# Two-layer transformer on one core: in its last stage, comparisons move to GpSimd and products and Gelus change places

## The reference, cut to what matters

```python
def _L1_ffn_ref(inputs, bn_gamma, bn_beta, w_q, keys_p, down, up):
    ...                                  # xn: inputs normed over all rows
    q = (xn @ w_q.T).reshape(b, s, 2, NH, KD).transpose(2, 0, 1, 3, 4)
    sim = jnp.einsum('pbnhd,hkpd->pbnhk', q, keys_p)
    scores, idx = jax.lax.top_k(sim, K)
    all_scores = (scores[0][..., :, None] + scores[1][..., None, :]).reshape(b, s, NH, K * K)
    all_idx = (idx[0][..., :, None] * NK + idx[1][..., None, :]).reshape(b, s, NH, K * K)
    sc, pk = jax.lax.top_k(all_scores, K)
    indices = jnp.take_along_axis(all_idx, pk, axis=-1)
    wd = down[indices]
    hmid = jnp.einsum('bnd,bnhkd->bnhk', inputs, wd)
    hmid = jax.nn.sigmoid(sc) * jax.nn.gelu(hmid, approximate=False)
    wu = up[indices]
    return jnp.einsum('bnhk,bnhkd->bnd', hmid, wu)
```

## Time and profile before

| what | us |
|---|---|
| median of 3 runs (590.31 to 592.97) | 590.48 |
| the profiled execution | 589.03 |
| its span | 587.3 |
| DVE busy | 490.6 |
| PE busy | 411.7 |
| ACT busy | 317.9 |
| POOL busy | 189.2 |

### The profile page before, as it was taken

One profiled execution on the slowest core, in us unless ns is written; L12 is line 12 of the kernel. 1 busy time (PEld: TensorE's weight loads), 2 busy tenths in 40 slices (PEclk: granted clock), 3 DMA queues, 4 the chain that ended last, 5 costly groups with the idle time before them and its releaser, 6 DMA issues. The chain is left out here.

```text
span 587.3 us, 12452 instructions
## 1 busy us (share of the span) xinstructions
PE 411.7 (70%) x4560; PEld 291.7 (50%) x4560; DVE 490.6 (84%) x2056; ACT 317.9 (54%) x639; POOL 189.2 (32%) x211
## 2 busy tenths in 40 slices
PE   1769869986998779854574637576847676767585
PEld 0455548644865467532473214353725354545475
DVE  3586699898999899987854799699979999999991
ACT  0602565346533664314641537767586868688591
POOL 4550224823194416813482230303030303030000
PEclk9998987698859976887755955685959595957577
DMA  7220000000000000000000000000000000000000
GB/s 200 73 61 0 1 2 2 2 1 0 2 0 3 0 2 1 2 1 0 1 2 0 2 1 1 2 2 11 2 10 2 12 2 11 2 11 1 12 2 19
DMA packets 12459, 6.72 MB, mean 11 GB/s; under 512 B 3182, under 2 KB 11758, under 8 KB 12398
## 3 DMA queue, kind: packets, MB, share of 16 engines
q1 hardware_dynamic: 10566, 4.34, 2.8%
q10 hardware_dynamic: 1832, 1.58, 1.0%
HBM read 4.87 MB, written 1.05 MB: 10 GB/s over the span
## 5 line engine op out<-in xcount | busy, mean ns | idle before, releaser
L1665 ACT ACTIVATE hot_last<-iota_f,lo_last 128x128 f16<-128x128 f32 x256 | 75.8, 388 | 0.3 <-DVE lo_last L1789 0.3
L1806 DVE TENSOR_TENSOR hot_lo<-lo_t,iota_lo 128x4096 f16<-128x4096 f16 x24 | 53.6, 2286 | 0.3
L1927 PE MATMUL psum<-hot_w,hot_lo 128*128 128x16 f16 x1536 | 43.6, 172 | 14.0 <-DVE hot_lo L1806 14.0
L1927 PEld LDWEIGHTS psum<-hot_w,hot_lo 128*128 128x128 f16 x1536 | 41.9, 101 | 20.6 <-DVE hot_lo L1806 19.6
L1893 PE MATMUL psum<-x3t,down_t 128*128 128x512 f32 x64 | 42.6, 768 | 13.3 <-ACT hid L1631 11.6
L1579 POOL TENSOR_TENSOR eq<-eq,side_f 128x1024 f16<-128x1024 f16 x14 | 28.9, 2083 | 55.5 <-DVE eq L1767 55.5
L1267 PE MATMUL psum<-q_hi,k_t 32*128 32x128 f16 x256 | 38.0, 259 | 9.8 <-DVE masked L883 6.4
L1587 POOL TENSOR_TENSOR rstd<-rstd,minus_half 128x2 f32<-128x2 f32 x8 | 5.6, 701 | 114.0 <-DVE rstd L1836 114.0
L622 POOL TENSOR_TENSOR s_lo<-masked,s_hi 128x512 f16<-128x512 f32 x32 | 36.5, 1170 | 16.5 <-ACT s_hi L463 12.8
L1736 DVE FIND_INDEX8 side_i<-side,keysims 128x8 uint32<-128x32 f32 x256 | 41.5, 185 | 0.0
L1196 PE MATMUL psum<-we,x1t 128*128 128x512 f32 x64 | 40.1, 777 | 0.4 <-DVE z L822 0.4
(11 more groups left out here) (265 smaller groups left out, 1186.2 us busy)
## 6 DMA issues: line engine op xcount, KB each, us to landing
xall<-in_L_attn_x SPq DMA_DIRECT2D x4, 256.0 KB, 6.9
out<-o SPq DMA_DIRECT2D x8, 128.0 KB, 1.9
we<-in_L_ffn_We SPq DMA_DIRECT2D x1, 512.0 KB, 4.0
downn<-in_L_ffn_down SPq DMA_DIRECT2D x1, 512.0 KB, 5.4
upw<-in_L_ffn_up SPq DMA_DIRECT2D x1, 512.0 KB, 6.5
wh<-in_L_attn_W_h SPq DMA_DIRECT2D x1, 256.0 KB, 4.5
keysn<-in_L_ffn_keys_p ACTq DMA_DIRECT2D x1, 256.0 KB, 10.9
wqkv<-in_L_attn_w_qkv ACTq DMA_DIRECT2D x1, 192.0 KB
```

Of the source, the lines that this page charges most:

```text
L1665: ins = nc.scalar.activation(hot_last[:, lane], iota_f[:], ACT.Abs, bias=lo_last[:, lane:lane + 1], scale=-1.0)
L1806: nc.vector.tensor_tensor(hot_lo[:, pairs], bc(lo_t[:, lanes].rearrange("p (j s) -> p j s", s=2).unsqueeze(2), [P, LB // 2, P, 2]), bc(v.i ...
L1927: ins = nc.tensor.matmul(bank[2 + q][:, c:c + 2 * EH], low, hot_w[:, i, lane // 2, :, :, lane % 2].rearrange("p t e -> p (t e)"), start=(i ...
```

## The change

POOL makes the comparisons: for each k of 0 to 7 one instruction on row and column of a whole pair, then two products. The tiles `eq` and `side_f` get k as their outer dimension for it, and PE's `decoded` starts when the first half is there. For the last pair DVE makes comparison and product over the whole pair. On DVE `residual` moves behind `rows_columns`, on POOL `numbers` ahead of `root`, on ACT `normal` behind the sigmoids. The 8 products of batch 1 and their Gelus move to the head of the stage, into six banks, and the first key scores move ahead in PE's list there. In later pairs ACT's three early Gelus stand between the lanes of the last one-hots, behind lanes 10, 20 and 30, and PE's third early product behind the first quarter.

```diff
     def H_BANK(b, c):
-        return (7, 2, 3, 4, 5, 0, 1, 7)[c] if b == 0 else 7
+        return ((7, 2, 3, 4, 5, 0, 1, 7), (2, 3, 4, 5, 0, 7, 2, 3))[b][c] if b < 2 else 7
+
+
+    H_FREE = ((0,) * 7 + (1,), (2, 3, 4, 5, 6, 8, 9, 10))
 
...
-        side_f = sb("side_f", [P, 4, 2, K, NH], F16)
+        side_f = sb("side_f", [P, 2, K, 2, 2, NH], F16)
...
-        eq = sb("eq", [P, 2, K, 2, HK], F16)
+        eq = sb("eq", [P, K, 2, 2, HK], F16)
...
-                def numbers(u):
-
-                    wait(pool, side_f_ok, u)
-                    wait(pool, eq_is, u)
-                    hit = eq[:, :, :, u % 2].rearrange("p i r (h k) -> p (i r) h k", k=K)
-                    nc.gpsimd.tensor_tensor(
-                        hit, hit, bc(side_f[:, u % 4].rearrange("p i r h -> p (i r) h").unsqueeze(3), [P, 2 * K, NH, K]),
-                        ALU.mult)\
-                        .then_inc(eq_ok.h, 1)
+                def numbers(p):
+
+
+                    wait(pool, rc16_ok, p)
+                    wait(pool, side_f_ok, 2 * p + 1)
+                    if p:
+                        wait(pool, dec_mm, p - 1)
+                    for half in range(2):
+                        r = slice(K // 2 * half, K // 2 * (half + 1))
+                        for k in range(r.start, r.stop):
+                            ins = nc.gpsimd.tensor_scalar(eq[:, k], rc16[:], float(k), None, ALU.is_equal)
+                        ins.then_inc(eq_is.h, 1)
+                    for half in range(2):
+                        r = slice(K // 2 * half, K // 2 * (half + 1))
+                        hit = eq[:, r].rearrange("p r i u (h k) -> p (r i u h) k", k=K)
+                        pool.wait_ge(eq_is.h, 2 * p + half + 1)
+                        nc.gpsimd.tensor_tensor(
+                            hit, hit, bc(side_f[:, p % 2, r].rearrange("p r i u h -> p (r i u h)").unsqueeze(2),
+                                         [P, K // 2 * 4 * NH, K]), ALU.mult).then_inc(eq_ok.h, 1)
...
                 for p in range(-1, PAIRS):
+                    if p + 2 < PAIRS:
+                        numbers(p + 1)
                     if p >= 1:
                         root(p - 1)
                     if p + 2 < PAIRS:
-                        for u in (2 * p + 2, 2 * p + 3):
-                            numbers(u)
                         for u in (2 * p + 4, 2 * p + 5):
                             candidates(u)
...
-                def last_one_hots(p):
...
+                def last_one_hots(p, meanwhile):
...
                     act.wait_ge(lo_last_ok.h, p + 1)
                     for lane in range(LB):
                         ins = nc.scalar.activation(hot_last[:, lane], iota_f[:], ACT.Abs, bias=lo_last[:, lane:lane + 1],
                                                    scale=-1.0)
+                        if lane % 10 == 9 and lane // 10 < len(meanwhile):
+                            hidden(p // PB + 1, meanwhile[lane // 10])
...
                 for p in range(-1, PAIRS):
-                    ahead = p >= 0 and p // PB + 1 < B
+                    ahead = p >= PB and p // PB + 1 < B
...
-                    if ahead:
-                        for c in HID_EARLY[p % PB]:
-                            hidden(p // PB + 1, c)
...
                     if p >= 0:
-                        last_one_hots(p)
-                    if p >= 1:
-                        normal(p - 1)
+                        last_one_hots(p, HID_EARLY[p % PB] if ahead else ())
                     for u in (2 * p + 2, 2 * p + 3):
                         if p < 0:
                             key_scores(u + 2)
                         if p >= 0 and u + 2 < TILES:
                             key_scores(u + 2)
+                    if p < 0:
+                        for c in range(EH):
+                            hidden(1, c)
                     if p + 1 < PAIRS:
                         for u in (2 * p + 2, 2 * p + 3):
                             sigmoids(u)
+                    if p >= 1:
+                        normal(p - 1)
                     if ahead:
...
-                def which_side(u):
-
-                    dve.wait_ge(rc16_ok.h, u // 2 + 1)
+                def last_numbers(p):
+
...
+                    dve.wait_ge(rc16_ok.h, p + 1)
+                    wait(dve, side_f_ok, 2 * p + 1)
+                    step(nc.vector.tensor_tensor(eq[:].rearrange("p r i u k -> p r (i u k)"), bc(places, [P, K, 4 * HK]),
+                                                 bc(v.iota_k[:].unsqueeze(2), [P, K, 4 * HK]), ALU.is_equal))
...
                     nc.vector.tensor_tensor(
-                        eq[:, :, :, u % 2], bc(rc16[:, u % 2].unsqueeze(2), [P, 2, K, HK]),
-                        bc(iota_r[:].unsqueeze(1), [P, 2, K, HK]), ALU.is_equal).then_inc(eq_is.h, 1)
-
-                def last_numbers():
-
-
-                    for u in (TILES - 2, TILES - 1):
-                        wait(dve, side_f_ok, u)
-                        wait(dve, eq_is, u)
-                        hit = eq[:, :, :, u % 2].rearrange("p i r (h k) -> p (i r) h k", k=K)
-                        ins = nc.vector.tensor_tensor(
-                            hit, hit, bc(side_f[:, u % 4].rearrange("p i r h -> p (i r) h").unsqueeze(3), [P, 2 * K, NH, K]),
-                            ALU.mult)
-                    ins.then_inc(eq_last_ok.h, 1)
+                        hit, hit, bc(side_f[:, p % 2].rearrange("p r i u h -> p (r i u h)").unsqueeze(2),
+                                     [P, K * 4 * NH, K]), ALU.mult).then_inc(eq_last_ok.h, 1)
...
-                nc.vector.tensor_copy(iota_r[:], bc(v.iota_k[:].unsqueeze(2), [P, K, HK]))
...
-                    if p >= 1:
-                        residual(p - 1)
                     if p + 1 < PAIRS:
                         for u in (2 * p + 2, 2 * p + 3):
                             second_choice(u)
                         rows_columns(p + 1)
-                    if p + 1 < PAIRS:
-                        for u in (2 * p + 2, 2 * p + 3):
-                            which_side(u)
+                    if p >= 1:
+                        residual(p - 1)
                     if p + 1 == PAIRS - 1:
-                        last_numbers()
+                        last_numbers(p + 1)
                     if p >= 0:
...
-                    if b == 0 and c == EH - 1:
-                        pe.wait_ge(h_ok.h, 1)
-                    elif b:
+                    if b >= 2:
                         pe.wait_ge(h_ok.h, EH * b + c)
+                    elif H_FREE[b][c]:
+                        pe.wait_ge(h_ok.h, H_FREE[b][c])
...
-                    else:
-                        wait(pe, eq_ok, 2 * p + 1)
-                    wait(pe, sig_ok, 2 * p + 1)
...
-                    for i, scaled in enumerate((ident_row, ident_h)):
-                        for r in range(K):
-                            nc.tensor.matmul(bank[1][:, 0:P], eq[:, i, r].rearrange("p t k -> p (t k)"), scaled[:],
+                    for r in range(K):
+                        if r % (K // 2) == 0 and p < PAIRS - 1:
+                            pe.wait_ge(eq_ok.h, 2 * p + 1 + r // (K // 2))
+                        for i, scaled in enumerate((ident_row, ident_h)):
+                            nc.tensor.matmul(bank[1][:, 0:P], eq[:, r, i].rearrange("p t k -> p (t k)"), scaled[:],
                                              start=(i == 0 and r == 0), stop=(i == 1 and r == K - 1))
+                    wait(pe, sig_ok, 2 * p + 1)
...
+                    elif q == 0:
+                        pe.wait_ge(h_ok.h, 2 * EH)
...
-                for c in range(4):
-                    hidden(0, c)
-                for u in (0, 1):
-                    key_scores(u)
-                for c in range(4, EH):
+                hidden(0, 0)
+                hidden(0, 1)
+                key_scores(0)
+                hidden(0, 2)
+                key_scores(1)
+                for c in range(3, EH):
                     hidden(0, c)
                 for u in (2, 3):
                     key_scores(u)
+                for c in range(EH):
+                    hidden(1, c)
                 pe.wait_ge(ident_ok.h, 1)
                 decoded(0)
...
-                    ahead = p // PB + 1 < B
-                    if ahead:
-                        for c in HID_EARLY[p % PB]:
-                            hidden(p // PB + 1, c)
-                    for q in range(QB - 1):
+                    ahead = p >= PB and p // PB + 1 < B
+                    early = HID_EARLY[p % PB] if ahead else ()
+                    for c in early[0:2]:
+                        hidden(p // PB + 1, c)
+                    gathered(p, 0)
+                    for c in early[2:3]:
+                        hidden(p // PB + 1, c)
+                    for q in range(1, QB - 1):
                         gathered(p, q)
```

(11 more changed lines are left out.)

10 lines of the change are left out of this document (5 added, 5 removed).

## The result

The changed kernel took 595.92 us (median of 9 runs, 594.55 to 599.22), the kernel before 590.48 beside it (9 runs); the ratio is 1.0092, with a 95% interval of 1.0066 to 1.0117. Predicted were 576.2 and faster. It is slower by about 0.9%.

The account below looks back on a forecast made before the run. DVE was taken to bound the kernel, with waits in some pairs from ACT's late one-hots. Head -1.1, first pair -5.6, second -1.4, third to sixth -7.1, last +0.9 sum to -14.3: 576.2 us, range 570.5 to 583.5.

Parts of the forecast that it names:

- The price of a comparison on POOL: POOL's eight comparisons a pair: 0.45 us each from start to start, with ends at 0.30 and 0.66.
- rival B: POOL faster than assumed: at 0.36 or less a comparison DVE bounds all four pairs; 572.4 us at 0.30; chance 0.22.
- The chain behind the numbers: Pairs three to six: root, normal, table load, Gelu and decoding follow POOL's numbers; next `lo_last` at 28.8 us, a 0.6 wait.
- Rival D: POOL comparisons past the turning point of 0.74 us make the kernel slower, +9 (599 us) at 0.9; chance 0.05.
- C: POOL slower, 0.56 to 0.74 us a comparison, binding the first and second pair too; 586.3 us at 0.66; chance 0.12.
- my account of ACT's lanes: Pairs three to six: ACT's last one-hots no longer bind, PE done by 19.7 us at most, fourth `mix` due at 19.15.
- First search earlier by 1.7: Head of the stage: key scores behind four PE matmuls instead of eight let DVE's search start 1.7 us earlier.
- Batch 1 at the head at no cost: Head: batch 1's products (7 to 9 us) and Gelus (4 us) fit where PE waited for POOL, if ended by about 346.
- rival E: PE slow in the head, 16 matmuls at 0.88 instead of 0.43: +4 on the forecast, 580 us; chance 0.09.
- First pair -5.6: First pair: 32.69 less 1.29 of comparisons and 4.28 of waiting for PE gives 27.1 us.
- Last pair's numbers +0.9: Last pair: comparison and product stay on DVE in a form with an innermost repeated operand, costing 0.9 us more.
- F: Gelus between lanes reload tables, 1.28 us each way, losing 2 to 7 in each of p = 2 to 5; no chance of its own.

Follow-up runs that it names:

- the probe: Kernel before, with instructions of several kinds added on POOL behind its last root, DVE idle; a comparison of 256 numbers took 854 ns.
- The two order experiments: Changed kernel, with the late Gelu ahead of normal on ACT: 589.85 us; or with residual and root back in their old places: 590.61 us.
- `cmp_dve`: Changed kernel with the comparisons back on DVE, as eight instructions a pair with a constant: 584.01 us, ratio to the kernel before 0.9907.
- `cmp_tt`: Changed kernel with all comparisons on DVE, in two two-input instructions a pair against a table: 583.85 us, ratio to the kernel before 0.9890.
- `cmp_tt_res`: `cmp_tt` with residual back ahead of the second choice on DVE: 580.40 us, ratio to the kernel before 0.9818.
- both shared forms: Changed kernel, DVE comparing with 0 to 3 and POOL with 4 to 7: 577.81 us; with the late Gelu ahead of normal in addition: 576.85 us.
- `head_only`: Kernel before with only the head changed (first key scores earlier, batch 1's products and Gelus there): 586.05 us, ratio 0.9929.

## Why the prediction was wrong

**What bounds the kernel before, and where its time is**: right. DVE bounds it, and with the comparisons off POOL's chain the rest of the change gained.

**The price of a comparison on POOL** is the step that failed: "I take 0.45 from start to start, nearest to `heads_t` ... ends 0.30 and 0.66". It measured 0.87 from start to start (6.95 for eight). The row was nearest in form, but has another pair of operations, which runs at another rate; and the upper end came from two-input rows on the belief that one input can't cost more. Both were beliefs about the engine, not rows of this operation. The Trainium skill's rule ("GPSIMD Engine Reference", 3.1, 1.03 cycles per element up to two operations), which I had with rival B, is off by more: 2.5 ns a number in the probe is 3 cycles at the 1.2 GHz it names.

**The chain behind the numbers** (root, normal, table load, Gelu, decoding): right, link by link. With 6.95 for 3.6 and 3.81 for 4.13 in it, 28.8 becomes 31.8, and the pairs took 31.81. (The products got shorter because DVE's comparison no longer runs beside the first.) The two order experiments took out the links it names.

**Rival D** is what happened, by its own mechanism; it had the turning point at 0.74 and +9 at 0.9. At 0.87 its 5.6 for each 0.1 give +7.3, less 2.2 for the shorter products in seven blocks, +5.1; measured is +5.4. I gave it 0.05, "it needs twice the nearest row", which is the same wrong row counted again.

**The signs that I named.** Waits over 2 at `lo_last` in every pair were to show C or D. They came in five of the eight; the third and fourth pair's are 1.52 and 1.28, the eighth's is 0.79. A wait left at the fourth `mix` was to show that my account of ACT's lanes is wrong. It is left in the third pair, 2.39: the account had ACT's lanes wait for nothing, and left out that `hidden` on PE stands behind the output products and so behind normal and root. With POOL on time it holds: in `cmp_dve`, `cmp_tt`, `cmp_tt_res` and both shared forms the waits there are 0.1 or less up to the seventh pair.

**The other terms.** First search earlier by 1.7: right, the idle time before it fell from 5.25 to 3.65 and it starts 6.34 behind the statistics (8.04 before):

```profile
326.41 1.58 DVE L1748 MAX8 side<-keysims 128x8 f32<-128x32 f32 x16 [3.65 <-ACT keysims L1637]
```

Batch 1 at the head at no cost: right in the changed kernel, where the products took 8.82 beside POOL's comparisons, so rival E did not come; not right without them, 1.29 in `head_only`. First pair -5.6: without POOL's comparisons it is 28.34 in `cmp_tt`, 1.29 of it comparison, so -5.6 is borne out. Last pair's numbers +0.9: right, 24.97 for 24.01. Gelus between lanes: no table reload but the one foreseen (F rightly dropped). Residual behind `rc16` I costed at its 0.95 alone; with POOL's products beside it, it costs 0.9 more.

## What to carry to other kernels

Before work moves to an engine, price the very operation there, in its form of operands: a row of another operation on the same engine was off by a factor of nearly two, and the two-input row was no ceiling. Then count what stands behind the moved work on its new engine and who waits for it; that sum, with the right price in it, gave the time of the third to sixth pair to 0.1 us each. Where the price is high, share the work between the two engines until both end together, instead of moving all of it.
